# Second attention: the value products of four units in one run, two banks and two engines for the turned probabilities, inverse sums transposed

## The reference

```python
q, k, v = (proj(q_w), proj(k_w), proj(v_w))          # 16 heads of 8 channels
scores = jnp.einsum('bhid,bhjd->bhij', q, k) / scale
scores = scores + alibi[None]
scores = jnp.where(causal[None, None], scores, -jnp.inf)
attn = jax.nn.softmax(scores, axis=-1)
out = jnp.einsum('bhij,bhjd->bhid', attn, v)
out = out.transpose(0, 2, 1, 3).reshape(b, l, D_MODEL)
return out @ o_w
```

## Time and profile before

| | |
|---|---|
| median of three runs | 2518.97 us |
| span of the profiled execution | 2521.2 us |
| first and last score product of this stage | 1975.5 and 2509.5 us |
| TensorE, VectorE, ScalarE busy over the span | 90%, 76%, 69% |
| instructions | 90789 |

### The profile page before, as it was taken

The page is one execution under the profiler, slowest core; times in us unless marked ns, Lnnn a source line. Parts: engine busy times, 40 slices in busy tenths (PEclk is TensorE's granted clock), DMA queues, the critical chain, the costliest instruction groups (busy, mean ns, idle before and its releaser), DMA issues. The chain is left out here.

```text
span 2521.2 us, 90789 instructions
## 1 busy us (share of the span) xinstructions
PE 2267.4 (90%) x34592; PEld 1784.8 (71%) x34592; DVE 1915.6 (76%) x7571; ACT 1737.9 (69%) x5614; POOL 841.7 (33%) x911
## 2 busy tenths in 40 slices
PE   6999998799889899888989989879999699999998
PEld 5888887577777777777777777557878466666665
DVE  6777773567777777777777777658888588888888
ACT  2333332677777777777777777866666599999988
POOL 3666665021111111111111212221121556556452
PEclk9999998899999999999999999989999799999999
DMA  7857442666666666666667764023322111111110
GB/s 242 237 157 193 115 111 51 162 162 162 168 171 171 171 168 171 165 168 168 164 165 175 170 166 116 14 72 111 106 98 78 38 35 35 31 37 34 30 36 14
DMA packets 360773, 304.79 MB, mean 121 GB/s; under 512 B 25368, under 2 KB 328856, under 8 KB 358952
## 3 DMA queue, kind: packets, MB, share of 16 engines
q1 hardware_dynamic: 349864, 271.93, 42.5%
q0 software_dynamic: 10496, 27.28, 3.6%
HBM read 166.43 MB, written 132.69 MB: 119 GB/s over the span
## 5 line engine op out<-in xcount | busy, mean ns | idle before, releaser
L823 ACT ACTIVATE probs<-neg_scores,low 128x256 f32<-128x256 f32 (+1 forms) x1152 | 574.2, 500 | 240.3 <-DVE low L959 226.4
L959 DVE CUSTOM_DVE_ANT_0 neg_scores<-scores,rel_bias 128x256 f32<-128x256 f32 x1024 | 373.6, 421 | 248.3 <-PE scores L1122 118.2
L1136 PE MATMUL probsT<-consts,probs 128*128 128x128 f32 x2240 | 360.6, 284 | 52.7 <-ACT probsT_s L839 48.2
L1136 PEld LDWEIGHTS probsT<-consts,probs 128*128 128x128 f32 x2240 | 248.1, 142 | 108.5 <-ACT probsT_s L839 68.5
L774 POOL TENSOR_SCALAR q_heads<-q_raw,consts,q_bias 128x256 f32<-128x256 f32 x128 | 69.2, 553 | 749.1 <-ACT q_raw L805 749.0
L1686 DVE CUSTOM_DVE_ANT_0 neg_scores<-scores,alibi 128x128 f32<-128x128 f32 (+1 forms) x896 | 266.1, 353 | 62.4 <-PE scores L1742 58.6
L275 POOL TENSOR_TENSOR hid<-hid,gate_bc 128x512 f32<-128x512 f32 x160 | 205.5, 1289 | 152.3 <-DVE hid L448 141.9
L301 ACT ACTIVATE ga<-gate_up 128x512 f32<-128x512 f32 x160 | 95.6, 597 | 224.4 <-PE gate_up L514 214.1
L967 DVE COPY rel_s<-scores 128x768 f32<-128x768 f32 x256 | 243.9, 953 | 4.4 <-PE scores L1122 3.1
L1648 ACT ACTIVATE probs<-neg_scores,low 128x128 f32<-128x128 f32 (+1 forms) x448 | 199.5, 447 | 55.6 <-DVE low L1686 46.6
L1112 PE MATMUL scores<-k_sides,q_heads 32*128 32x256 f32 (+1 forms) x2304 | 206.1, 424 | 25.7 <-DVE rel_s L967 20.0
(11 more groups left out here) (205 smaller groups left out, 4977.9 us busy)
## 6 DMA issues: line engine op xcount, KB each, us to landing
rel_rows<-rel_s SPq DMA_DIRECT2D x256, 192.0 KB
rel_bias<-rel_rows SPq DMA_DIRECT2D x256, 192.0 KB, 3.4
gate_bc<-gate_rows SPq DMA_DIRECT2D x32, 1024.0 KB, 10.2
rel_rows<-rel_s SPq DMA_DIRECT2D x256, 128.0 KB
rel_bias<-rel_rows SPq DMA_DIRECT2D x256, 128.0 KB, 3.1
packed<-ffn_in SPq DMA_DIRECT2D x8, 1280.0 KB, 15.1
xe<-packed SPq DMA_DIRECT2D x16, 640.0 KB, 3.9
expert_out<-ye POOLq DMA_DIRECT2D x16, 640.0 KB, 3.2
```

Source lines behind the costliest of these rows:

```text
L823: act.activation(probs[s % 3][:, j, 0:w], neg[s % 2][:, j, 0:w], ACT.Exp, bias=low[s % 3][:, j:j + 1], scale=-1.0, accum_out=sums[s // UB ...
L959: dve.tensor_tensor_reduce(neg[s % 2][:, j, 0:w], S_ps[:, 512 * j:512 * j + w], bias_of(s)[:, j, :] if s < NU0 else alibi[:, 4 * j + s % 4 ...
L1136: ins = pe.transpose(PT_ps[:, j * P:(j + 1) * P], probs[u % 3][:, j, kt * P:(kt + 1) * P], ident)
```

## The change

- `probsT` has two buffers of four units each in place of three of one unit.
- A narrow unit with an odd number is turned into bank 1, and ScalarE copies it out. Even narrow units stay in bank 0 with VectorE. Wide units use both banks as before. The semaphores count by bank (`moved[k]`).
- `value` of single units is gone. `values(g)` does the products of all four units of a group in one run, after the `score` of a step s that leaves 2 divided by 4. `valued` counts groups.
- The inverse sums are turned by a transpose (L1781 after the change) in place of a product with the identity.
- In a step, the projections come before `score` instead of after it.

The norm's place in VectorE's order, at the head of the steps that leave 3 divided by 4, is not changed, nor are the rules for the exponentials. The numbers in the edited lines follow from the above.

```diff
-            probsT = [sbb(f"probsT1_s{i}", [P, KT, 4, P]) for i in range(3)]
+            probsT = [sbb(f"probsT1_s{i}", [P, 4, KT, 4, P]) for i in range(2)]
...
+            def bank_of(u, kt):
+                return kt if half_of(u) else u % 2
+
+            def moved_before(u, k):
+                return sum(1 for v in range(u) for kt in range(half_of(v) + 1) if bank_of(v, kt) == k)
+
+            def turned_with(u, kt):
+                return u + wide_before(u) + kt + 1
...
-                            act.wait_ge(valued, UB * (b - 1))
+                            act.wait_ge(valued, 2 * (b - 1))
...
-                    if 0 <= u < NU1 and half_of(u) == 1:
-                        act.wait_ge(turned, u + 1 + wide_before(u + 1))
-                        if u >= 3:
-                            act.wait_ge(valued, u - 2)
-                        act.copy(probsT[u % 3][:, 1, :, :].rearrange("p g q -> p (g q)"), PT_ps[1][:, :]).then_inc(moved1, 1)
+                    if 0 <= u < NU1 and (half_of(u) or u % 2):
+                        kt = half_of(u)
+                        act.wait_ge(turned, turned_with(u, kt))
+                        if u >= UB:
+                            act.wait_ge(valued, u // 4 - 1)
+                        act.copy(probsT[u // 4 % 2][:, u % 4, kt, :, :].rearrange("p g q -> p (g q)"), PT_ps[1][:, :]).then_inc(moved[1], 1)
...
-                        dve.wait_ge(valued, 4 * (g + 1))
+                        dve.wait_ge(valued, g + 1)
...
+                    if 0 <= u < NU1 and (half_of(u) or u % 2 == 0):
+                        dve.wait_ge(turned, turned_with(u, 0))
+                        if u >= UB:
+                            dve.wait_ge(valued, u // 4 - 1)
+                        dve.tensor_copy(probsT[u // 4 % 2][:, u % 4, 0, :, :].rearrange("p g q -> p (g q)"), PT_ps[0][:, :]).then_inc(moved[0], 1)
                     if 0 <= u < NU1:
-                        dve.wait_ge(turned, u + 1 + wide_before(u))
-                        if u >= 3:
-                            dve.wait_ge(valued, u - 2)
-                        dve.tensor_copy(probsT[u % 3][:, 0, :, :].rearrange("p g q -> p (g q)"), PT_ps[0][:, :]).then_inc(moved0, 1)
                         if u % 4 == 3:
                             g = u // 4
                             dve.wait_ge(exped, 16 * (g + 1))
                             dve.reciprocal(rinv[:, :], sums[g % 2][:, :, :].rearrange("p j i -> p (j i)")).then_inc(one_inverse, 1)
                             dve.wait_ge(one_inverse, g + 1)
                             if g >= 1:
-                                dve.wait_ge(valued, 4 * g)
+                                dve.wait_ge(valued, g)
                             dve.tensor_copy(rinv_c[:, :, :], rinv[:, :].unsqueeze(2).to_broadcast((P, H, C))).then_inc(inverted, 1)
...
                 def turn(u):
                     pe.wait_ge(exped, 4 * (u + 1))
                     for kt in range(half_of(u) + 1):
-                        if kt == 0 and u >= 1:
-                            pe.wait_ge(moved0, u)
-                        if kt == 1 and wide_before(u):
-                            pe.wait_ge(moved1, wide_before(u))
+                        k = bank_of(u, kt)
+                        if moved_before(u, k):
+                            pe.wait_ge(moved[k], moved_before(u, k))
                         for j in range(4):
-                            ins = pe.transpose(PT_ps[kt][:, j * P:(j + 1) * P], probs[u % 3][:, j, kt * P:(kt + 1) * P], ident)
+                            ins = pe.transpose(PT_ps[k][:, j * P:(j + 1) * P], probs[u % 3][:, j, kt * P:(kt + 1) * P], ident)
                         ins.then_inc(turned, 1)
 
-                def value(u):
-                    b, g, i = u // UB, u // 4, u % 4
-                    pe.wait_ge(moved0, u + 1)
-                    if half_of(u):
-                        pe.wait_ge(moved1, wide_before(u + 1))
-                    if i == 0 and g >= 1:
+                def values(g):
+                    b, n = g // 2, g % 2 + 1
+                    for k in range(KT):
+                        pe.wait_ge(moved[k], moved_before(4 * g + 4, k))
+                    if g >= 1:
                         pe.wait_ge(normed, g)
-                    if u % UB == 0:
+                    if g % 2 == 0:
                         pe.wait_ge(spare_free, job_no["v", b])
-                    n = half_of(u) + 1
-                    for kt in range(n):
-                        for j in range(4):
-                            rows = slice(32 * j, 32 * j + 32)
-                            ins = pe.matmul(O_ps[rows, 0:P], v_of[b % 2][:, kt, i, rows], probsT[u % 3][:, kt, j, :],
-                                            start=(i == 0 and kt == 0), stop=(i == 3 and kt == n - 1), skip_group_check=True)
-                    if i == 3:
-                        pe.wait_ge(inverted, g + 1)
-                        ins = pe.matmul(O_ps[:, P:2 * P], rinv_c[:, :, :].rearrange("p h c -> p (h c)"), ident, start=True, stop=True)
-                    ins.then_inc(valued, 1)
+                    for i in range(4):
+                        for kt in range(n):
+                            for j in range(4):
+                                rows = slice(32 * j, 32 * j + 32)
+                                pe.matmul(O_ps[rows, 0:P], v_of[b % 2][:, kt, i, rows], probsT[g % 2][:, i, kt, j, :],
+                                          start=(i == 0 and kt == 0), stop=(i == 3 and kt == n - 1), skip_group_check=True)
+                    pe.wait_ge(inverted, g + 1)
+                    pe.transpose(O_ps[:, P:2 * P], rinv_c[:, :, :].rearrange("p h c -> p (h c)"), ident).then_inc(valued, 1)
 
                 for s in STEPS:
                     if 0 <= s - 2 < NU1:
                         turn(s - 2)
-                    if 0 <= s - 3 < NU1:
-                        value(s - 3)
+                    for name, b in jobs_at.get(s, ()):
+                        project(name, b)
                     if 0 <= s + 1 < NU1:
                         score(s + 1)
-                    for name, b in jobs_at.get(s, ()):
-                        project(name, b)
+                    g, r = divmod(s - 6, 4)
+                    if r == 0 and 0 <= g < 2 * NB:
+                        values(g)
```

More of the change, by code:

```diff
@@ L1488, in program @@
             turned = semb("probsT_ready")
-            moved0 = semb("probsT_first_half_moved")
-            moved1 = semb("probsT_second_half_moved")
+            moved = [semb(f"probsT_bank{k}_moved") for k in range(KT)]
             valued = semb("values_ready")
```

## The result

The changed kernel takes 2581.45 us (median of 4 runs, 2580.19 to 2583.5); the kernel before took 2516.53 us (median of 4 runs, three of which are those named above). The ratio is 1.0256, with a 95% interval of 1.0236 to 1.0276. The span of the profiled execution went from 2521.2 to 2579.8 us.

What follows compares the result with a forecast made beforehand. No engine is full; a ring of waits between TensorE's score products and VectorE's `neg_scores` decides. Terms 1.16 + 1.17 + 0 - 0.13 = +2.20 us a block, times 28 blocks = 62 us, giving 2581 us; range 2564 to 2603 us.

Steps and rivals of the forecast that it cites:

- The run in front of the norm: Gaps before units 7 and 3: the norm waits for the group's whole value run, +1.16 and +1.17 us a block.
- The transposed inverse sums: From last value product to norm: one instruction less leaves 0.32 us of 0.46, bounds 0.15 and 0.46.
- Units 7 to 2: From the end of `neg_scores` 7 to unit 2: value products leave TensorE's chain, `qk` enters; 5.07 against 5.07 us, 0.
- the walk: Starts of `neg_scores` followed through one block in old and new order; the gaps sum to +2.20 us a block.
- The copy of unit 3: Gap before unit 6: this odd narrow copy leaves VectorE, 1.03 us becomes 0.90, -0.13 us a block.
- ScalarE's copies: Two added copies a block of 0.46 us, hidden by ScalarE's waits for units 3 and 7; uncovered they cost 0.92.
- The projections' case: `out` ahead of `score(6)` blocks it if ScalarE's copy-out of `v` is late: block +2.7 to +3.1, 2595 to 2606 us; 0.11.
- TensorE relieved: Rival: TensorE is the bound and the run saves it 1.1 us a block, 31 us, giving 2488 us; chance 0.05.
- the ring: `score(u+1)` waits for `neg_scores(u)`, `neg_scores(u+1)` for `score(u+1)`; queued work inside lengthens the block, work beside it does not.
- a sign of being wrong: The granted clock falling in TensorE's new waits, where every product would take longer than in the rows; no size given.

Runs made afterwards that it cites:

- The two experiments that move the wait aside: Changed kernel with the norm behind `neg_scores` and copy, 2530.05 us; changed kernel with values ahead of the score products, 2525.56 us.
- the spread order: Changed kernel with value products spread to where TensorE waits for VectorE, norms and projections moved, odd narrow copies on VectorE or ScalarE: 2530.3 and 2530.25 us.

## Why the prediction was right

- **The run in front of the norm** (+1.16 and +1.17): measured 2.70 - 1.46 = 1.24 and 3.35 - 2.08 = 1.27. The value run itself was sized well: 2245.35 to 2246.36 is 1.01 us (0.99 predicted), 2255.07 to 2256.95 is 1.88 (1.83). The two experiments that move the wait aside take back 51 and 56 us.
- **The transposed inverse sums**: 0.32 us to the norm was taken, 0.37 is in the rows (2246.36 to 2246.73). This and the run are the 0.15 us a block by which the sum was short.
- **Units 7 to 2** (0): -0.06. Two value products went, `qk` and the late second half of `turn(7)` came: ScalarE's copy starts at 2251.01, 2.38 us after the end of unit 7 as in the walk, and `qk` 3.48 after it, with 3.53 foreseen. With the projections behind the score products the block is 0.4 to 0.5 us shorter.
- **The copy of unit 3** (-0.13): -0.11 in the changed kernel. Alone in the kernel before it is nothing; the prediction's reason was too simple, as it did not ask what is late next there.
- **ScalarE's copies**: hidden, as predicted. Undoing or adding them alone was tried in the kernel before and in the spread order, where they cost nothing; in the changed kernel ScalarE is busy 17.95 of 21.03 us and waits up to 2.0 us for VectorE in front of units 3 and 7. The runs with the norm moved are the exception: there ScalarE is nearly full (1.04 us idle of 19.14, 0.16 of 18.20), and what its two added copies cost in them was not tried.
- **The projections' case** (0.11): TensorE does wait for `v` in front of `out`, 19 times by the waits above, but it is through in time; unit 6's gap is 0.92 us.
- **TensorE relieved** (0.05): it does work 1.04 us a block less, near the 1.1 of this rival, and all of that is idle time. The Trainium skill's rule that a change of tiling mode drains TensorE (TensorEngine Tiling (Array Packing), section Tiling Modes) fits the run, in which 16 instructions more than x16 cost 0.44 us and no 0.15 between units. But the time saved was not in the ring.

The agreement of the times (2581.0 and 2581.45) is closer than the working deserves; part of it is luck. The forecast was +61.6 us, and in the spans, where the parts can be read, it is +58.6. The ordinary blocks were 0.15 us longer than forecast, 4 us in all. Single long blocks gave back 3.8: the clock took 5 us more in five of them (below), which the prediction had named as a sign of being wrong and not as a cost, while the one of 23.88 us and smaller ones went. The stage began 8 us earlier and ended 5 us later than two forecast blocks explain; neither was in a term. The start is scatter: the first `qk` comes between 1961.8 and 1974.2 us in the 13 traces, and no run edits what comes before it. In the changed kernel TensorE waits for `query_heads` twice (6.1 us) and both times at the start of the stage, against five times (12.8 us) before. That a longer block gives POOL time for it was in no term.

## What to carry to other kernels

Work that is batched in one engine's queue must be followed to the instruction that waits for its end on another engine, and to what stands behind that instruction: here the norm was not moved, and so it put a run of 1.0 or 1.9 us between two steps of a ring. A batch belongs where the ring has its idle time, or its reader behind the ring's next step. Before an order is moved, each other queue that waits on the moved work is to be read as well, slow ones like POOL's included; and where two engines' chains end together, as in front of unit 7 here, a gain on one of them alone was nothing.

## What was not expected of the hardware

TensorE's granted clock fell in five of the 24 blocks of the changed kernel that follow the two at the stage's start (where it was 0.79 and 0.92), each time at the score products of unit 5 or just behind them. Each of these five blocks has a granted clock of 0.92 and is 21.96 to 21.99 us long, about 0.94 more than 21.03. On TensorE in one of them:

```profile
2173.48 0.71 PE L1752 MATMUL scores<-kT,q_heads 32*128 32x256 f32 x8 [0.66 <-DVE low L1695]
2174.12 0.66 PE L1763 MATMUL probsT<-consts,probs 128*128 128x128 f32 x4
2175.78 0.76 PE L1752 MATMUL scores<-kT,q_heads 32*128 32x256 f32 x8 [1.00 <-DVE low L1695]
2176.48 1.11 PE L1763 MATMUL probsT<-consts,probs 128*128 128x128 f32 x4
2177.38 1.18 PE L1739 MATMUL projected<-weights,ctxT 128*128 128x128 f32 x4
2178.49 1.24 PE L1752 MATMUL scores<-kT,q_heads 32*128 32x256 f32 x8
```

and over 5.6 us there (columns as above):

```profile
2175.00:2180.60 5.60, 4.82 (x32) 3.35 (x32) 3.99 (x22) 5.02 (x21) 0.00 (x0) 0.70 0.01 3
```

Four transposes that take 0.66 us in other blocks take 1.11, `out` 1.18 instead of 0.71, the score products 1.24 instead of 0.71: that is the lower of the two levels, 1.2 GHz. Ahead of it TensorE waited 1.00 us for VectorE, and before that 0.66. But the ordinary blocks have these waits too, and keep their clock:

```profile
2216.76 0.71 PE L1752 MATMUL scores<-kT,q_heads 32*128 32x256 f32 x8 [0.67 <-DVE low L1695]
...
2219.07 0.71 PE L1752 MATMUL scores<-kT,q_heads 32*128 32x256 f32 x8 [1.00 <-DVE low L1695]
```

The run with the norm moved has the wait of 1.00 us as well, and its granted clock is 1.00 from 2004 to 2484 us:

```profile
2204.49 0.71 PE L1752 MATMUL scores<-kT,q_heads 32*128 32x256 f32 x8 [1.00 <-DVE low L1686]
```

So these two waits alone do not bring the clock down. What it costs can be read: 5 x 0.94, about 5 us. In the kernel before no block behind the first two has a lower clock but the one of 23.88 us; its five others that are longer by 0.1 to 0.7 us, 1.9 us together, are at a clock of 1.00. At the end of the changed kernel the clock is at the lower level twice more (0.53 from 2538.0 to 2541.6 us, 0.51 from 2558.6 to 2565.6). TensorE idles 4.5 of 21.03 us in the changed kernel and 1.1 of 18.68 before; that this is what brings the clock down was not tried.
